# Softmax numerators kept in fp32 against an fp32 value table in a two-layer attention kernel

## The chip, the cores and the metric

The kernel runs on one core of one Trainium2 chip. The metric is the device time of one execution in microseconds (us); the engines meant below are PE (TensorE, with its weight loads shown apart as PEld), DVE (VectorE), ACT (ScalarE), POOL (GpSimd) and SP (SyncE, which here only issues transfers).

## The reference

Two batches of 1024 rows with 256 features pass through two layers. Each layer is an attention of 16 heads (16 features a head) over 77 keys, and then a feed-forward part. The part that matters here is the attention:

```python
attn = jax.nn.softmax(jnp.einsum('bqhd,bkhd->bhqk', q, k) * scale, axis=-1)   # layer 0
out = jnp.einsum('bhqk,bkhd->bqhd', attn, v).reshape(B, T_q, D_MODEL)
...
scores = scores + distance_bias[:, None, :, :]                                # layer 1
attn = jax.nn.softmax(scores, axis=-1)
out = jnp.einsum('bhqk,bkhd->bhqd', attn, v)
```

Layer 0's feed-forward part is a pair of products with ternary weights (256 to 1024 to 256, with GELU); layer 1's is one dense expert of the same sizes with ReLU, followed by a layer norm.

## The kernel before

**Units.** The 2048 rows are worked in 8 units of 256 rows (`NU = 8`, `UR = 256`). The program is written engine by engine, with semaphores between the engines; each engine runs its instructions strictly in the written order.

**Slots.** A layer's attention is a software pipeline, written out in `attn_slot(l, s)` on every engine. Slot `s` computes the score maxima of unit `s`, the scores and exponentials of unit `s-1` (three of five parts, the other two in slot `s+1`), the values product of unit `s-2`, the transposed outputs and the output projection of unit `s-3`, and the layer norm's factors and what follows for unit `s-4`. Within a slot six steps `r = 0..5` interleave these. On PE the slot ends with `values(l, s-2, 0)`, the transposes of the maxima (`shifts_transposed`), and `values(l, s-2, 1)`. Layer 0's last slots are interleaved with the ternary part, and layer 1's first three slots with the end of it; layer 1's last slots are interleaved with the expert (`expert_hidden`, `expert_out`), which then runs alone to the end.

**Heads packed by keys.** The 8 heads of a half have 8 x 77 = 616 key columns, padded to 5 tiles of `KR = 124` (`TPH = 5`). A part `r` of the scores is two such tiles by 256 rows, `psD`, 124 x 512. Both halves make 10 tiles, 5 parts a unit.

**Numerators, before.** ACT writes the exponential of a part to `p32` (a ring of four parts, L716), and copies it to fp16, `ph` (`high`, L725). POOL subtracts and rounds the rest to fp16, `pl` (`plo`, L498). `exponent` waits until POOL has read the ring's slot (`plo` of part n-4); `high` and `plo` wait until the values product of unit u-2 is done (`ppv`), since `ph` and `pl` are double buffered by unit. The profile's names for them are `p`, `pp_hi` and `pp_lo`.

**Values product.** The numerators are the stationary operand (124 x 128), and a small table of values (124 x 34 or 124 x 51: two or three heads of 16 features and a column for the sum) is the moving one. The table too is split in two fp16 parts, `vo` and `vlo`, written by DVE in `tables_v` (L938). For each of two groups of 128 rows there are 10 tiles with three products each, L1431, L1433 and L1434: 60 matmuls a unit.

**What follows.** DVE divides (`divide`, L1099 and L1100), PE transposes (L1510), ACT and DVE split the result to fp16 halves (L674, L1128), PE projects (L1448), DVE adds the residual (L1072) and takes the layer norm's statistics (L881 to L886), POOL computes the factors (`factors`, L400 to L417), ACT applies them (L689). In layer 0 DVE then works out the quantisation scales (L1045 to L1049). The scores' operand `qb` is laid out by transfers that SP issues (L293, L307), the last of them the shift rows from `mT` (L317), which come from the transposed maxima (PE L1520, ACT L707).

The fp16 halves of the numerators share their memory with the expert's hidden activations (`ehT`).

Of the kernel before, what the change touches and what calls it, by code (L numbers as in the profile page):

```python
# [23 lines left out]
ALU = mybir.AluOpType  # L24
# [45 lines left out]
def build(nc, io):  # L70
    es = ExitStack()
    with es:
# [68 lines left out]
        vo = sb("vo", [KR, B, 2, TPH, SLOTS, VW], F16)  # L141
        vlo = sb("vlo", [KR, B, 2, TPH, SLOTS, HD], F16)
# [21 lines left out]
        ehT = [t[:, 0:2 * FK * UR].rearrange("p (a c r) -> p a c r", a=2, c=FK) for t in pp]  # L164
# [74 lines left out]
        A = [Stage(f"a{l}", "pq pm pmT psc ppv poT pwo pxT qhi qlo mx mTc exp phi plo norm oTh oTl res fac app xn dq q1 xTh xTl")  # L239
# [134 lines left out]
        def _(pool):  # L374
# [115 lines left out]
            def plo(l, u, r):  # L490

                a = A[l]
                if not 0 <= u < NU:
                    return
                n = 5 * u + r
# [51 lines left out]
        def _(act):  # L547
# [162 lines left out]
            def exponent(l, u, r):  # L710

                a, n = A[l], 5 * u + r
                if 0 <= u < NU:
                    act.wait_ge(a["psc"], n + 1)
                    ge(act, a["plo"], n - 3)
                    a_(p32[:, n % 4, :, :], psD[n % 2][0:KR, :].rearrange("p (t r) -> p t r", t=2),  # L716
                       ACT.Exp, scale=1.0 / SSC).then_inc(a["exp"], 1)

            def high(l, u, r):

                a, n = A[l], 5 * u + r
                if 0 <= u < NU:
# [1032 lines left out]
```

## Time and profile before

| what | value |
|---|---|
| median of 3 runs | 428.0 us (427.83, 428.0, 437.11) |
| the profiled execution, its own time | 433.62 us |
| its span in the profile | 431.9 us |
| mean granted PE clock in it | 0.92 of full speed |
| instructions in the span | 9332 |

The busy times and the groups of instructions stand with the other rows further down. In the profile's timeline and lists a row gives the duration of an instruction as the profiler recorded it. PE's instructions are pipelined: a matmul record is some 0.18 us long even where the next one starts 0.025 us later, so the pace of a run of matmuls is read from start to start, never from the mean length.

### The profile page before, as it was taken

What the parts mean: (1) busy time and instruction counts of PE and PEld (TensorE: products, weight loads), DVE (VectorE), ACT (ScalarE), POOL (GpSimd) and SP (SyncE); (2) the same over time, 40 slices, a digit from 0 to 9 for tenths busy, and PEclk for the clock granted to TensorE, in tenths of its full rate; (3) what the DMA queues carried; (4) which work ended last, traced back from release to release, by engine and by line L of the source; (5) the groups of instructions that cost most, each with busy time, mean ns of one, the idle gap of its engine ahead of it and who ended that gap; (6) DMA issues with size and microseconds to landing.
All of it is one profiled execution on the core that took longest, in us unless ns stands there. A gap on an engine that the chain in (4) does not pass through costs nothing.

```text
span 431.9 us, 9332 instructions
## 1 busy us (share of the span) xinstructions
PE 333.7 (77%) x3346; PEld 269.8 (62%) x3346; DVE 309.8 (72%) x663; ACT 282.7 (65%) x515; POOL 233.1 (54%) x414
## 2 busy tenths in 40 slices
PE   4858657876768656757866689999868899999990
PEld 4636445765655334444654568777767789888880
DVE  6965726888887776799977553678866648777775
ACT  2147666878988668997952675877677655555520
POOL 4664554366778511457664744765587144544443
PEclk9986766899999689888989998999999999999996
DMA  8965122111110000000054222221100000000001
GB/s 237 278 93 180 27 62 77 29 30 30 39 40 22 0 2 1 2 0 2 8 153 128 48 50 49 49 49 44 44 11 2 2 2 27 26 26 25 26 26 49
DMA packets 34213, 21.48 MB, mean 50 GB/s; under 512 B 10359, under 2 KB 33528, under 8 KB 34091
## 3 DMA queue, kind: packets, MB, share of 16 engines
q1 hardware_dynamic: 32440, 20.41, 17.6%
q10 hardware_dynamic: 1728, 0.47, 0.8%
q8 instruction: 27, 0.44, 0.4%
q14 instruction: 18, 0.15, 0.1%
HBM read 10.34 MB, written 2.10 MB: 29 GB/s over the span
## 4 chain that ended last, share of the span: by engine, by line
PE 32%; DVE 26%; ACT 13%; issue 10%; POOL 7%; SPq 6%; ACTq 2%; DMA 2%; POOLq 0%; DVEq 0%
PE psA L1681 8%; PE psD L1666 4%; SPq L293 4%; PE psBE L1666 4%; DVE st L881 3%; DVE mx L1114 3%; ACT pp_hi L725 2%; DVE ham L1160 2%; POOL lns L400 2%; PE psA L1467 2%; PE psA L1448 2%; ACTq L585 2%; PE psD L1379 2%; ACT p L716 1%; DVE o L1100 1%
## 5 line engine op out<-in xcount | busy, mean ns | idle before, releaser
L498 POOL TENSOR_TENSOR pp_lo<-p,pp_hi 124x512 f16<-124x512 f32 x80 | 92.5, 1176 | 60.1 <-ACT pp_hi L725 59.9
L400 POOL TENSOR_TENSOR lns<-lns,mhalf 128x2 f32<-128x2 f32 x40 | 31.3, 782 | 114.0 <-DVE lns L886 113.7
L1114 DVE TENSOR_REDUCE mx<-psBE 128x6 f32<-128x462 f32 (+1 forms) x96 | 54.5, 579 | 31.4 <-PE psBE L1405 31.2
L716 ACT ACTIVATE p<-psD 124x512 f32<-124x512 f32 x80 | 47.7, 598 | 36.2 <-PE psD L1379 32.0
L1379 PE MATMUL psD<-qb,ktb 98*124 98x256 f16 (+1 forms) x256 | 49.4, 290 | 5.2 <-DMA qb<-mT 3.6
L725 ACT ACTIVATE pp_hi<-p 124x512 f16<-124x512 f32 x80 | 50.4, 630 | 0.0
L1379 PEld LDWEIGHTS psD<-qb,ktb 98*124 98x124 f16 (+1 forms) x256 | 34.1, 145 | 9.4 <-DMA qb<-mT 6.7
L1405 PE MATMUL psBE<-kt_hi,q_hi 128*128 128x308 f16 (+2 forms) x128 | 34.7, 313 | 4.1 <-DVE mx L1114 2.7
L1431 PE MATMUL psA<-vo,pp_hi 124*128 124x34 f16 (+1 forms) x320 | 28.0, 183 | 11.1 <-DVE xT_lo L906 4.8
L1681 PE MATMUL psA<-ew_hi,pp_lo 128*128 128x256 f16 x128 | 34.9, 273 | 0.0
L1681 PE MATMUL psA<-ew_hi,pp_hi 128*128 128x256 f16 x128 | 34.9, 273 | 0.0
L1681 PE MATMUL psA<-ew_lo,pp_hi 128*128 128x256 f16 x128 | 34.9, 273 | 0.0
L1431 PEld LDWEIGHTS psA<-vo,pp_hi 124*128 124x128 f16 x320 | 26.0, 97 | 14.2 <-issue 14.1
L1199 DVE TENSOR_TENSOR pp_lo<-space,pp_hi 128x512 f16<-128x512 f32 x32 | 23.4, 750 | 15.5 <-ACT space L827 15.4
L571 ACT ACTIVATE xT_hi<-psA 128x512 f16<-128x512 f32 x24 | 14.2, 593 | 23.2 <-PE psA L1285 23.2
L825 ACT ACTIVATE pp_hi<-psD,b1s 128x256 f16<-128x256 f32 x32 | 15.7, 491 | 19.7 <-PE psD L1666 19.7
L1434 PE MATMUL psA<-vo,pp_lo 124*128 124x34 f16 (+1 forms) x320 | 27.9, 182 | 0.0
L1433 PE MATMUL psA<-vlo,pp_hi 124*128 124x32 f16 (+1 forms) x320 | 27.8, 181 | 0.0
L881 DVE BATCH_NORM_STATS2 st<-xs 128x6 f32<-128x256 f32 x64 | 23.8, 414 | 3.0 <-DMA xs<-in_x 2.7
L1433 PEld LDWEIGHTS psA<-vlo,pp_hi 124*128 124x128 f16 x320 | 25.6, 97 | 0.3
L1376 PE MATMUL psD<-bb,selb 128*124 128x256 f16 x80 | 21.5, 279 | 5.2 <-DMA qb<-mT 5.2
L1434 PEld LDWEIGHTS psA<-vo,pp_lo 124*128 124x128 f16 x320 | 25.5, 97 | 0.0
(203 smaller groups left out, 1109.9 us busy)
## 6 DMA issues: line engine op xcount, KB each, us to landing
qb<-q_hi SPq DMA_DIRECT2D x128, 32.0 KB
xs<-in_x SPq DMA_DIRECT2D x8, 256.0 KB, 5.2
tw_raw<-in_tw SPq DMA_DIRECT2D x2, 1024.0 KB, 8.8
qb<-q_lo SPq DMA_DIRECT2D x64, 32.0 KB
space<-in_ew SPq DMA_DIRECT2D x2, 1024.0 KB, 6.5
out<-space SPq DMA_DIRECT2D x8, 256.0 KB, 2.1
qb<-bT_lo SPq DMA_DIRECT2D x8, 104.0 KB
space<-in_distN SPq DMA_DIRECT2D x1, 616.0 KB
```

Of the source, the lines that this page charges most:

```text
L400: nc.gpsimd.tensor_tensor(lns[:, n % 4, 1, :], lns[:, n % 4, 0, :], mhalf[:, :], ALU.pow).then_inc(s_rs, 1)
L498: nc.gpsimd.tensor_tensor(pl[:, u % 2, 2 * r:2 * r + 2, :], p32[:, n % 4, :, :], ph[:, u % 2, 2 * r:2 * r + 2, :], ALU.subtract).then_inc( ...
L716: a_(p32[:, n % 4, :, :], psD[n % 2][0:KR, :].rearrange("p (t r) -> p t r", t=2), ACT.Exp, scale=1.0 / SSC).then_inc(a["exp"], 1)
L725: a_(ph[:, u % 2, 2 * r:2 * r + 2, :], p32[:, n % 4, :, :], ACT.Copy).then_inc(a["phi"], 1)
L881: i = v.bn_stats(st[:, n % 4, j, :], src[:, j, :])
L1114: v.tensor_reduce(mx[:, s % 2, j * H + 6 * k:j * H + 6 * k + hn], psBE[:, n % 2, 0:hn * KEYS].rearrange("p (h k) -> p h k", h=hn), AX.X, A ...
L1379: i = mm(o, ktb[0:rows, hf * B + b, g, (t - g) * KR:(t - g + 1) * KR], qb[0:rows, u % NQ, hf, g, :], start=first, stop=(k == 1 and g == mi ...
L1405: i = mm(psBE[:, n % 2, o0 * KEYS:(o0 + c1 - c0) * KEYS], q[0][:, u % 2, hf, j * 128:(j + 1) * 128], kt[:, hf, b, c0 * KEYS:c1 * KEYS], st ...
L1431: mm(o, p_, w.rearrange("p s c -> p (s c)"), start=(hf == 0 and t == 0), stop=False, skip_group_check=True)
L1433: mm(ov[:, :, 0:HD], p_, wl, start=False, stop=False, skip_group_check=True)
L1434: i = mm(o, pl[:, u % 2, hf * TPH + t, rows_], w.rearrange("p s c -> p (s c)"), start=False, stop=(hf == 1 and t == TPH - 1), skip_group_c ...
L1681: i = mm(o, ehT[x_][:, u % 2, c, j * 128:(j + 1) * 128], ew2[w_][:, c, :], start=(j == 0 and c == 0 and x_ == 0 and w_ == 0), stop=(j == 1 ...
```

## The change

The numerators stay in fp32. ACT's exponential writes straight to a buffer of two units (`pp`, 2 x 10 tiles x 256 rows, whose rows 0 to 123 are `p32`), the fp16 copy on ACT and the subtraction on POOL are gone, and with them the semaphores `phi` and `plo`. The values table is one fp32 table, `vo`, and `vlo` is gone. The values product is one matmul of fp32 by fp32 for each tile and group of rows: 20 a unit. `exponent` now waits for `ppv` of unit u-2, and `values` for the five exponentials. The expert's `ehT` becomes a view of the same buffer.

```diff
-        vo = sb("vo", [KR, B, 2, TPH, SLOTS, VW], F16)
-        vlo = sb("vlo", [KR, B, 2, TPH, SLOTS, HD], F16)
+        vo = sb("vo", [KR, B, 2, TPH, SLOTS, VW])
...
-        p32 = sb("p32", [KR, 4, 2, UR])
-        pp = [sb(f"pp_{p}", [128, 2 * 2 * TPH * UR], F16) for p in ("hi", "lo")]
-        ph, pl = [t[0:KR, :].rearrange("p (a t r) -> p a t r", a=2, t=2 * TPH) for t in pp]
+        pp = sb("pp", [128, 2, 2 * TPH * UR])
+        p32 = pp[0:KR, :, :].rearrange("p a (t r) -> p a t r", t=2 * TPH)
...
-        ehT = [t[:, 0:2 * FK * UR].rearrange("p (a c r) -> p a c r", a=2, c=FK) for t in pp]
+        ehT = [pp[:, :, i * FK * UR // 2:(i + 1) * FK * UR // 2].bitcast(F16).rearrange("p a (c r) -> p a c r", c=FK)
+               for i in (0, 1)]
...
-            def plo(l, u, r):
-                ...
-                pool.wait_ge(a["phi"], n + 1)
-                ge(pool, a["ppv"], 2 * (u - 1))
-                nc.gpsimd.tensor_tensor(pl[:, u % 2, 2 * r:2 * r + 2, :], p32[:, n % 4, :, :],
-                                        ph[:, u % 2, 2 * r:2 * r + 2, :], ALU.subtract).then_inc(a["plo"], 1)
...
-                plo(l, s - 2, 2)
                 if 0 <= s - 4 < NU:
                     factors_act((1 + 2 * l) * NU + s - 4, (1.0, SX)[l], A[l]["fac"])
-                for u, r in ((s - 2, 3), (s - 2, 4), (s - 1, 0), (s - 1, 1)):
-                    plo(l, u, r)
...
                     act.wait_ge(a["psc"], n + 1)
-                    ge(act, a["plo"], n - 3)
-                    a_(p32[:, n % 4, :, :], psD[n % 2][0:KR, :].rearrange("p (t r) -> p t r", t=2),
+                    ge(act, a["ppv"], 2 * (u - 1))
+                    a_(p32[:, u % 2, 2 * r:2 * r + 2, :], psD[n % 2][0:KR, :].rearrange("p (t r) -> p t r", t=2),
                        ACT.Exp, scale=1.0 / SSC).then_inc(a["exp"], 1)
-
-            def high(l, u, r):
-                ...
-                    act.wait_ge(a["exp"], n + 1)
-                    ge(act, a["ppv"], 2 * (u - 1))
-                    a_(ph[:, u % 2, 2 * r:2 * r + 2, :], p32[:, n % 4, :, :], ACT.Copy).then_inc(a["phi"], 1)
...
-                for p in (0, 1):
-                    src = (psG, psX)[l][0:KR, p * 240:(p + 1) * 240].rearrange("p (t s d) -> p t s d", t=TPH, s=SLOTS)
-                    i = v.tensor_tensor((vo, vlo)[p][:, b, hf, :, :, 0:HD], src,
-                                        vm[:, :, :].unsqueeze(3).to_broadcast([KR, TPH, SLOTS, HD]), ALU.mult)
+                src = (psG, psX)[l][0:KR, 0:240].rearrange("p (t s d) -> p t s d", t=TPH, s=SLOTS)
+                v.tensor_tensor(vo[:, b, hf, :, :, 0:HD], src,
+                                vm[:, :, :].unsqueeze(3).to_broadcast([KR, TPH, SLOTS, HD]), ALU.mult).then_inc(s_vo, 1)
...
-                    pe.wait_ge(a["phi"], 5 * u + 5)
-                    pe.wait_ge(a["plo"], 5 * u + 5)
+                    pe.wait_ge(a["exp"], 5 * u + 5)
...
-                        p_ = ph[:, u % 2, hf * TPH + t, rows_]
-                        mm(o, p_, w.rearrange("p s c -> p (s c)"), start=(hf == 0 and t == 0), stop=False,
-                           skip_group_check=True)
-                        mm(ov[:, :, 0:HD], p_, wl, start=False, stop=False, skip_group_check=True)
-                        i = mm(o, pl[:, u % 2, hf * TPH + t, rows_], w.rearrange("p s c -> p (s c)"), start=False,
+                        i = mm(psV[:, j, h0 * VW:(h0 + hn) * VW], p32[:, u % 2, hf * TPH + t, rows_],
+                               vo[:, b, hf, t, 0:hn, :].rearrange("p s c -> p (s c)"), start=(hf == 0 and t == 0),
                                stop=(hf == 1 and t == TPH - 1), skip_group_check=True)
```

No instruction changes its place beside the others; what is gone leaves the rest in order. On PE, the first tiles of the first values product of layer 0 (unit 0, rows 0 to 127) stood so before, right behind the last score maxima of the slot; `psA` holds the output, `pp_hi` and `pp_lo` are the fp16 halves, and the semaphores waited for stand in brackets:

```order
130 L1405 MATMUL psBE<-kt_hi,q_hi 128x308 [waits mx_a0]
131 L1431 MATMUL psA<-vo,pp_hi 128x34 [waits plo_a0,xTl_l0,phi_a0,s_vo]
132 L1433 MATMUL psA<-vlo,pp_hi 128x2x16
133 L1434 MATMUL psA<-vo,pp_lo 128x34
134 L1431 MATMUL psA<-vo,pp_hi 128x51
135 L1433 MATMUL psA<-vlo,pp_hi 128x3x16
136 L1434 MATMUL psA<-vo,pp_lo 128x51
```

The same place with the change, where `pp` is the fp32 buffer:

```order
130 L1379 MATMUL psBE<-kt_hi,q_hi 128x308 [waits mx_a0]
131 L1400 MATMUL psA<-vo,pp 128x34 [waits xTl_l0,exp_a0,s_vo]
132 L1400 MATMUL psA<-vo,pp 128x51
133 L1400 MATMUL psA<-vo,pp 128x34
134 L1400 MATMUL psA<-vo,pp 128x51
135 L1400 MATMUL psA<-vo,pp 128x34 x2
```

Nothing moved; three matmuls of a tile became one, and the waits for `phi` and `plo` became one for the exponentials.

On ACT, a stretch of slot 5 of layer 0 before, from the copy `xT_hi` (step 1) to the first of the two normalisations (step 3):

```order
95 L743 ACTIVATE xT_hi<-psA,epsc 128x2x256 [waits pxT_a0]
96 L716 ACTIVATE p<-psD 124x512 [waits plo_a0,psc_a0]
97 L725 ACTIVATE pp_hi<-p 124x512 [waits ppv_a0,exp_a0]
98 L674 ACTIVATE oT_hi<-psA 128x512 [waits pwo_a0,poT_a0]
99 L600 ACTIVATE wo_hi<-wspace 128x512 [waits d_wo1]
100 L716 ACTIVATE p<-psD 124x512 [waits plo_a0,psc_a0]
101 L725 ACTIVATE pp_hi<-p 124x512 [waits ppv_a0,exp_a0]
102 L689 ACTIVATE xn<-xs,lns 128x256 [waits fac_a0]
```

and with the change:

```order
71 L719 ACTIVATE xT_hi<-psA,epsc 128x2x256 [waits pxT_a0]
72 L701 ACTIVATE pp<-psD 124x512 [waits ppv_a0,psc_a0]
73 L659 ACTIVATE oT_hi<-psA 128x512 [waits pwo_a0,poT_a0]
74 L585 ACTIVATE wo_hi<-wspace 128x512 [waits d_wo1]
75 L701 ACTIVATE pp<-psD 124x512 [waits ppv_a0,psc_a0]
76 L674 ACTIVATE xn<-xs,lns 128x256 [waits fac_a0]
```

The copies to `pp_hi` are gone from between the others, and the exponential has taken over their wait for `ppv`.

## Rows read from the trace of the kernel before

**Rows 1.** The page: busy time, share and instructions of each engine.
```profile
PE 333.7 (77%) x3346; PEld 269.8 (62%) x3346; DVE 309.8 (72%) x663; ACT 282.7 (65%) x515; POOL 233.1 (54%) x414
```

**Rows 2.** Stages: start:end, length, busy PE, PEld, DVE, ACT, POOL, clock, DMA share, GB/s.
```profile
58.00:71.00 13.00, 7.32 (x88) 6.40 (x89) 7.00 (x17) 8.90 (x17) 4.82 (x5) 0.67 0.14 38
...
109.00:121.00 12.00, 9.51 (x126) 7.97 (x125) 10.26 (x24) 11.03 (x22) 8.14 (x12) 1.00 0.15 36
...
285.40:297.35 11.95, 11.14 (x135) 9.07 (x134) 9.51 (x20) 8.47 (x18) 7.54 (x13) 1.00 0.18 42
```

**Rows 3.** The page's groups for what the change removes (busy, mean ns, idle before).
```profile
L498 POOL TENSOR_TENSOR pp_lo<-p,pp_hi 124x512 f16<-124x512 f32 x80 | 92.5, 1176 | 60.1 <-ACT pp_hi L725 59.9
L725 ACT ACTIVATE pp_hi<-p 124x512 f16<-124x512 f32 x80 | 50.4, 630 | 0.0
```

**Rows 4.** DVE's table writes (L938): count, shortest, median, longest ns.
```profile
L938 DVE TENSOR_TENSOR vlo<-psA,vm x8: 390/394/398, 35.2 to 217.8; 124x240 f16<-124x240 f32 x8
```

**Rows 5.** Timeline of PE, layer 0, first and last value matmul of a half.
```profile
90.30 0.18 PE L1431 MATMUL psA<-vo,pp_hi 124*128 124x34 f16 x1 [0.91 <-ACT pp_hi L725]
...
91.03 0.18 PE L1434 MATMUL psA<-vo,pp_lo 124*128 124x34 f16 x1
91.78 0.44 PE L1520 MATMUL psBE<-id,mx 128*128 128x128 f32 x2 [0.56 <-DVE mx L1114]
```

**Rows 6.** Weight loads of four kinds: count, shortest/median/longest ns, first and last start.
```profile
L1433 PEld LDWEIGHTS psA<-vlo,pp_hi x320: 95/96/151, 60.8 to 337.9; 124*128 124x128 f16 x160
...
L1510 PEld LDWEIGHTS psA<-id,o x64: 137/141/231, 70.2 to 339.6; 128*128 128x128 f32 x64
...
L1311 PEld LDWEIGHTS psA<-wspace,ctxT x16: 143/148/149, 15.2 to 135.0; 128*77 128x77 f32 x16
...
L1297 PEld LDWEIGHTS psA<-ctxT,wspace x16: 188/239/338, 5.4 to 122.3; 128*128 128x128 f32 x16
```

**Rows 7.** Timeline of PEld at full clock: start, length of the run, what, count.
```profile
120.35 0.47 PEld L1510 LDWEIGHTS psA<-id,o 128*128 128x128 f32 x4
...
121.42 1.09 PEld L1297 LDWEIGHTS psA<-ctxT,wspace 128*128 128x128 f32 x8
...
212.58 0.36 PEld L1330 LDWEIGHTS psA<-vsp_hi,selb 77*124 77x124 f16 x5 [0.88 <-issue]
212.86 0.36 PEld L1330 LDWEIGHTS psA<-vsp_lo,selb 77*124 77x124 f16 x5
```

**Rows 8.** Critical chain, layer 1: two places of a stretch that is all PE.
```profile
265.71 1.31 PE psA L1448 x12
...
269.95 0.24 PE psD L1379 x2
```

**Rows 9.** Timeline of PE, layer 1: where it waits, in brackets, before a row.
```profile
259.65 0.32 PE L1376 MATMUL psD<-bb,selb 128*124 128x256 f16 x1 [2.17 <-DMA qb<-mT]
...
286.09 0.27 PE L1467 MATMUL psA<-xT_hi,wq_hi 128*128 128x256 f16 x1 [0.59 <-DVE xT_lo L906]
...
290.17 0.18 PE L1431 MATMUL psA<-vo,pp_hi 124*128 124x34 f16 x1 [0.18 <-ACT pp_hi L725]
```

**Rows 10.** Critical chain of layer 1, one slot apart.
```profile
290.17 0.74 ACT q_hi L666 x2
...
297.35 0.72 POOL lns L400
...
302.08 0.74 ACT q_hi L666 x2
```

**Rows 11.** Quantisation scale in layer 0 (DVE L1049): shortest/median/longest ns.
```profile
L1049 DVE TENSOR_SCALAR dq<-am,ws x8: 209/998/1007, 90.3 to 173.1; 128x2 f32<-128x2 f32 x8
```

**Rows 12.** Timeline of ACT and of PE in layer 0's third slot.
```profile
55.31 0.60 ACT L716 ACTIVATE p<-psD 124x512 f32<-124x512 f32 x1 [3.43 <-POOL pp_lo L498]
...
60.84 0.19 PE L1431 MATMUL psA<-vo,pp_hi 124*128 124x34 f16 x1 [4.81 <-DVE xT_lo L906]
...
63.42 0.88 PE L1285 MATMUL psA<-id,xn 128*128 128x128 f32 x3
```

More of the change, by code:

```diff
@@ L231, in __getitem__ @@
                 return self.s[n]
-        A = [Stage(f"a{l}", "pq pm pmT psc ppv poT pwo pxT qhi qlo mx mTc exp phi plo norm oTh oTl res fac app xn dq q1 xTh xTl")
+        A = [Stage(f"a{l}", "pq pm pmT psc ppv poT pwo pxT qhi qlo mx mTc exp norm oTh oTl res fac app xn dq q1 xTh xTl")
              for l in (0, 1)]
@@ L487, in _ @@
             diag(id16, 1.0)
-            def plo(l, u, r):
[L492 to L495, printed above, removed]
-                pool.wait_ge(a["phi"], n + 1)
-                ge(pool, a["ppv"], 2 * (u - 1))
-                nc.gpsimd.tensor_tensor(pl[:, u % 2, 2 * r:2 * r + 2, :], p32[:, n % 4, :, :],
-                                        ph[:, u % 2, 2 * r:2 * r + 2, :], ALU.subtract).then_inc(a["plo"], 1)
             def attn_slot(l, s):
-                plo(l, s - 2, 2)
                 if 0 <= s - 4 < NU:
                     factors_act((1 + 2 * l) * NU + s - 4, (1.0, SX)[l], A[l]["fac"])
-                for u, r in ((s - 2, 3), (s - 2, 4), (s - 1, 0), (s - 1, 1)):
-                    plo(l, u, r)
             for s in range(NU + 4):
@@ L737, in attn_slot @@
                         exponent(l, u, k)
-                        high(l, *((u, k - 1) if k > 0 else (u - 1, 4)))
                     if r == 1 and 0 <= s - 5 < NU:
@@ L935, in tables_v @@
                 dve.wait_ge(s_vop, 4 * l + step)
-                for p in (0, 1):
-                    src = (psG, psX)[l][0:KR, p * 240:(p + 1) * 240].rearrange("p (t s d) -> p t s d", t=TPH, s=SLOTS)
-                    i = v.tensor_tensor((vo, vlo)[p][:, b, hf, :, :, 0:HD], src,
-                                        vm[:, :, :].unsqueeze(3).to_broadcast([KR, TPH, SLOTS, HD]), ALU.mult)
-                i.then_inc(s_vo, 1)
+                src = (psG, psX)[l][0:KR, 0:240].rearrange("p (t s d) -> p t s d", t=TPH, s=SLOTS)
+                v.tensor_tensor(vo[:, b, hf, :, :, 0:HD], src,
+                                vm[:, :, :].unsqueeze(3).to_broadcast([KR, TPH, SLOTS, HD]), ALU.mult).then_inc(s_vo, 1)
                 v.tensor_scalar(vo[:, b, hf, :, :, HD], vm[:, :, :], SM * SONE, None, ALU.mult).then_inc(s_vo, 1)
@@ L1329, in tables_vo @@
                         h0 = hf * HH + VH0[t]
-                        i = mm((psG, psX)[l][0:KR, p * 240 + t * 48:p * 240 + t * 48 + 48], sel[:, t * KR:(t + 1) * KR],
+                        i = mm((psG, psX)[l][0:KR, t * 48:t * 48 + 48], sel[:, t * KR:(t + 1) * KR],
                                vsp[p][:, b, h0 * HD:(h0 + SLOTS) * HD], start=(p == 0 and t == 0), stop=(p == 1 and t == TPH - 1))
@@ L1426, in values @@
                         h0, hn = hf * HH + VH0[t], VHN[t]
-                        o = psV[:, j, h0 * VW:(h0 + hn) * VW]
-                        ov = o.rearrange("p (s c) -> p s c", c=VW)
-                        w, wl = vo[:, b, hf, t, 0:hn, :], vlo[:, b, hf, t, 0:hn, :]
-                        p_ = ph[:, u % 2, hf * TPH + t, rows_]
-                        mm(o, p_, w.rearrange("p s c -> p (s c)"), start=(hf == 0 and t == 0), stop=False,
-                           skip_group_check=True)
-                        mm(ov[:, :, 0:HD], p_, wl, start=False, stop=False, skip_group_check=True)
-                        i = mm(o, pl[:, u % 2, hf * TPH + t, rows_], w.rearrange("p s c -> p (s c)"), start=False,
+                        i = mm(psV[:, j, h0 * VW:(h0 + hn) * VW], p32[:, u % 2, hf * TPH + t, rows_],
+                               vo[:, b, hf, t, 0:hn, :].rearrange("p s c -> p (s c)"), start=(hf == 0 and t == 0),
                                stop=(hf == 1 and t == TPH - 1), skip_group_check=True)
```

2 lines of the change are left out of this document (removed).

## The prediction

> **What bounds the kernel now.** I read the page's busy times first: no engine is full over the span; PE is busy 77%, DVE 72%, ACT 65%, POOL 54% [rows 1]. So the question is what sets the length of a slot, and for that I read three stretches of the table by stage [rows 2]. In a warm slot of layer 0 (109 to 121 us) ACT is busy 11.0 of 12.0 us, DVE 10.3, PE 9.5. In a slot of layer 1 (285.4 to 297.35) PE is busy 11.1 of 11.95 and nothing else is above 9.5. PE's record of a matmul is longer than its place in the pipeline, so I also count its work by pace. Twelve fp16 matmuls of 256 columns take 1.31 us, 0.109 each [rows 8]. A slot of layer 1 issues 26 such for the scores and 12 each for queries and projection (50 x 0.109 = 5.5 us), maxima of 4928 columns (2.1), ten fp32 transposes at about 0.11 (1.1; four loads take 0.47 with the last one's 0.14, [rows 6, 7]), and 60 value matmuls. Thirty of these run from 90.30 to 91.03, 0.025 us each, 1.5 for a unit [rows 5]. That is 10.2 us of 11.95. In layer 0 the same count gives 8.0, since the bias is not in its scores and maxima.
>
> The critical chain shows the loop of layer 1: from one copy of the queries at 290.17 to the next at 302.08 it is 11.9 us long, through DVE, POOL's factors (297.35) and ACT [rows 10]; PE waits in that slot for 0.59 and 0.18 us only [rows 9]. So PE is just under the bound there and a loop of small steps sits on it.
>
> **What goes.** POOL loses 80 subtractions of 1176 ns, 92.5 us, and ACT 80 copies of 630 ns, 50.4 us [rows 3], that is 5.9 and 3.15 us a unit. Little of it is on a path that lasts. Where it is: (a) in layer 0's third slot ACT stood 3.43 us for POOL's subtractions, and this reached PE's first values product, which started at 60.84 after 4.81 us of waiting [rows 12]; I take -3.3. (b) DVE's small scale product in layer 0 has a median of 998 ns and a shortest of 209 [rows 11], and its slow ones run beside POOL's subtractions, whose 1176 ns [rows 3] are near it; with those gone it may give back up to 0.8 us a unit, which goes into the layer 0 sum below. (c) DVE loses 8 table writes of 394 ns, 3.2 us [rows 4], partly under PE; with the few other small DVE steps I take -2. (d) ACT's copies before the values product: PE waits there 0.91 us in layer 0 [rows 5], 0.18 in layer 1 [rows 9].
>
> **What comes.** 20 fp32 matmuls a unit for 60 fp16 ones. No row shows an fp32 product of 128 loaded and 34 columns, so I build the price. First, how often the engine runs one. The key table's products are 8 calls in the program (4 a layer), and the profile has 16 loads of them [rows 6]: two loads and two passes a call. So a unit becomes 40 load and matmul pairs. Second, what a load costs. fp16 loads of 128 columns last 96 ns, fp32 ones of 77 columns 148, of 128 columns 188 at the least [rows 6]. The two fp32 forms differ by 40 ns for 51 columns, 0.8 ns a column; so 128 columns occupy 128 x 0.8 = about 105 ns beyond a fixed part of 85. The same fixed part leaves 11 ns for the fp16 load, which is why 0.025 apart is possible today. Third, whether loads hide. Five fp16 loads of 124 columns take 0.36 us and the next five start 0.28 behind the first [rows 7], so one comes each 0.055 us, with 48 moving columns each (one column at the pace above is 0.0004 us, so 0.02): the loads set the pace, and the moving part is hidden below them. So 40 x 0.108 = 4.3 us a unit at full clock, against 1.5: **+2.8 us a unit**, 16 units, +45 us of PE work. Lower bound: the fp32 transposes' pace of 0.11 for 128 columns with loads of 141 ns would leave 53 ns a load, 2.2 us a unit, +0.6. Upper bound: eight fp32 pairs of 154 columns start 0.129 apart [rows 7]; if load and moving part did not overlap at 34 to 51 columns, a pair would cost 0.105 + 0.035 = 0.14, 5.6 us a unit, +4.1. At half the clock a pair costs 0.21 (load of 338 ns at the longest, [rows 6]), 8.5 us a unit.
>
> The Trainium skill, page "FP8 and Floating Point Precision", section "TensorE Precision Notes", says that a true fp32 product makes four passes. If each had a load of its own, a unit would cost twice my 4.3 us and the change would be well over 40 us slower; the rows above show two loads a call. The page "TensorE: Matmul & The Clock Gate", section "Weight-path perf modes", says that the fast weight load needs 128 columns and an input that is not fp32, which speaks against this change; the gap between 96 and 188 ns agrees.
>
> **Where the +2.8 falls.** *Layer 0, unit 0:* at 60.84 to 63.42 the clock is low (0.67 over the stretch, [rows 2, 12]). The 2.6 us become up to 8.5; with the clock partly up, I take +5. *Unit 1:* +1.5. *Units 2 to 5:* the first half of the product ends before the last maximum of the slot does (PE waits 0.91 ahead of it and 0.56 behind, [rows 5]), so its +1.4 is hidden; the second half, ahead of the next slot's first maxima, adds 1.4. Against it stand (b) and the copies in ACT's full slots, about 1.4 a unit: 0 in sum. *Units 6 and 7:* +1, beside the ternary part. With (a): **layer 0 about +4**.
>
> *Layer 1, unit 0:* hidden, because PE stands 2.17 us for the shift rows' transfer [rows 9] and the chain runs through SP until then. *Unit 1:* from 259.65 to 270 the critical chain is PE alone [rows 8], +2.8. *Units 2 to 4:* PE's own count becomes 10.2 + 2.8 = 13.0 us a slot, with waits of about 0.4 say 13.4. The first of these slots begins inside the stretch without a gap, so I let it pay the whole +2.8; the others were 11.95: +1.4 each. *Unit 5:* no queries in its slot, +0.4. *Units 6 and 7:* +2.8 each on PE, less ACT's copies (3.15 a unit) ahead of the expert's first activations, together +1. From about 340 us on, PE runs the expert without a gap and nothing changes. **Layer 1 about +8.**
>
> **What costs nothing.** The exponential's new wait for `ppv` of unit u-2: PE issues the scores of unit u behind that product, so it is met whenever the scores are. If the order on PE were another, ACT would stand for up to the length of a product, 4.3 us a unit. The write of fp32 instead of fp16 by ACT has the length of L716 already. No transfer is added; SP's shift rows start when the transposed maxima are out, and what PE does meanwhile only becomes longer.
>
> **Sum.** 431.9 + 4 + 8 - 2 = 441.9 us of span, +2.3%. The profiled execution took 433.6, the median of the runs 428.0; 428.0 x 441.9 / 431.9 = **438 us**.
>
> **The rivals.** *Absorbed:* the loop without PE sets the slots, and relief on ACT, POOL and DVE (5.9 + 3.15 us a unit) pays for the PE work outside layer 1's middle slots. Then only units 1 to 4 of layer 1 cost (about +8) and the rest returns it: 428 to 434. For it: ACT's 11.0 of 12 us in layer 0. Against: PE's 13.0 us exceed 11.95. *Faster, by a cheap load:* if an fp32 load of a product costs what that of a transpose does (53 ns), PE gains 0.6 us a unit only, layer 1's slots stay at about 11.5, and (a) to (d) are left: -3 -2, some -0.5 a slot: 420. It decides at about 70 ns a pair, where PE's count meets 11.5. Against it stands the 188 ns row. *No overlap, or the clock:* at 0.14 us a pair each unit costs 1.3 us more, of which some 10 of 16 show: +13, 451. If the granted clock fell in the long runs of loads, where few columns move, one such stretch of 3.4 us in each of 12 slots would lose 1.7 us each: 458. Against: the clock is 1.00 in the slots of rows 2 with PE standing now and then.
>
> The Trainium skill, page "SBUF — State Buffer", section "Who interferes with whom", states that DVE and POOL block each other on a shared pair of ports; the 998 against 209 ns agree, and (b) would be worth all of its 0.8 us a unit by that rule, which would bring the time to about 434.
>
> **Chances.** As forecast (434 to 445) 0.45; absorbed 0.25; faster by the cheap load or by more relief than counted 0.12; no overlap or lower clock 0.18. A difference under 2% is about what a measurement of this kernel cannot tell from no change, so 419.4 to 436.6 is "same": the absorbed case, a quarter of the forecast's chance and a third of the faster case, 0.40; faster 0.08; slower 0.52. Range for 8 in 10: 424 to 454; the forecast's own is 434 to 445.
>
> **What would show it.** Right: 40 pairs a unit on PE, loads of about 190 ns, starts 0.108 apart; slots of layer 1 at 13.0 to 13.6 us with PE's waits under 0.5; DVE L1049 at 0.2; the expert's stretch as long as before. Wrong: pairs at 0.05 or 0.14 apart; PE waits as before in layer 1; a granted clock under 1.00 in layer 1's middle; slots in layer 0 shorter than 12 us, which would say that ACT's copies were the bound there.

## The result: slower by 5.9%, outside the predicted range

The changed kernel takes 456.5 us (median of four runs, 451.4 to 461.5) against 430.5 for the kernel before on the same chip: ratio 1.059, 95% interval 1.043 to 1.075. I had said 438, with 424 to 454 as the range. Executions over 1.5% above the fastest of their kernel (here 461.5) are left out of every ratio. The profiled execution took 456.45 us with a span of 454.7, 22.8 more than the span of before.

The page of the changed kernel first: busy times with instructions, the share of each engine in the chain that ended last, and the price of the new product (matmuls, then weight loads).

```profile
PE 392.7 (86%) x3026; PEld 333.6 (73%) x3026; DVE 295.0 (65%) x655; ACT 244.0 (54%) x435; POOL 140.2 (31%) x334
...
PE 64%; DVE 17%; ACT 5%; issue 4%; SPq 3%; POOL 2%; ACTq 2%; DMA 1%; DVEq 0%; POOLq 0%
...
L1400 PE MATMUL psA<-vo,pp 124*128 124x34 f32 (+1 forms) x640 | 80.8, 287 | 3.5 <-DVE xT_lo L882 3.5
...
L1400 PEld LDWEIGHTS psA<-vo,pp 124*128 124x128 f32 x640 | 80.7, 206 | 4.1 <-issue 3.8
```

Against [rows 1] POOL lost 93 us, ACT 39, DVE 15, and PE gained 59. In the chain PE had 32% before; now it has 64%. The 640 pairs are the 40 a unit that were forecast. Their loads have a median of 192 ns:

```profile
L1400 PEld LDWEIGHTS psA<-vo,pp x640: 186/192/338, 57.0 to 357.9; 124*128 124x128 f32 x160
...
L1023 DVE TENSOR_SCALAR dq<-am,ws x8: 207/208/208, 89.3 to 178.0; 128x2 f32<-128x2 f32 x8
```

The second row answers [rows 11]: DVE's small scale product is at its shortest time in all eight units.

Three slots follow, one of layer 0 and two of layer 1, in the columns of [rows 2] (start:end, length, busy PE, PEld, DVE, ACT, POOL, granted clock, DMA share, GB/s). Each runs from DVE's reciprocal of one unit's sums, about 1 us behind that unit's values product, to the next unit's. In the kernel before these slots were 12.75, 11.91 and 11.92 us long.

```profile
94.64:108.87 14.23, 14.23 (x100) 13.30 (x98) 9.50 (x23) 8.86 (x16) 2.44 (x7) 0.74 0.14 28
...
290.73:306.43 15.70, 15.70 (x116) 14.27 (x115) 9.23 (x21) 6.14 (x12) 1.90 (x7) 0.83 0.15 31
...
306.43:320.34 13.91, 13.91 (x119) 12.94 (x118) 9.13 (x20) 6.02 (x12) 1.89 (x7) 0.96 0.17 35
```

PE is busy for the whole of each. The new thing is the granted clock: 0.74, 0.83 and 0.96, where the second and third stretch of [rows 2] showed 1.00. The same table in pieces of 7 us, for PE alone (length, busy PE, clock, DMA share, GB/s), puts the fall in its place:

```profile
99.00:106.00 7.00, 7.00 (x65) 0.98 0.10 21
106.00:113.00 7.00, 7.00 (x36) 0.51 0.17 36
...
280.00:287.00 7.00, 7.00 (x65) 1.00 0.24 50
287.00:294.00 7.00, 7.00 (x33) 0.51 0.16 34
```

The clock is at 2.4 GHz in nearly all of the first piece and at 1.2 in nearly all of the second. The change falls into a values product, in layer 0 these rows of the weight loads' timeline (start, length of the run, count):

```profile
102.24 2.33 PEld L1400 LDWEIGHTS psA<-vo,pp 124*128 124x128 f32 x20
104.41 0.29 PEld L1487 LDWEIGHTS psBE<-id,mx 128*128 128x128 f32 x2
104.67 3.09 PEld L1400 LDWEIGHTS psA<-vo,pp 124*128 124x128 f32 x20
```

Ten such stretches stand in this kernel, each beginning in a values product or just behind it; six of the sixteen products have none. All in all PE is at half clock for about 103 us of the span, in the kernel before for 69 (twice the part of the mean granted clock that is missing, times the span: 0.887 of 454.7 us, 0.920 of 431.9). An estimate from these: 34 more microseconds at half speed are some 17 us of work lost, if PE is the bound in all of them. The kernel's own executions point the same way: 449.6 us of span went with a clock of 0.896, 454.7 with 0.887 and 454.8 with 0.881.

The chain of layer 1 answers [rows 10]: DVE, POOL, ACT and DMA are gone from it, and two slots read PE all through. Of that stretch:

```profile
298.50 1.31 PE psA L1415 x12
...
300.08 2.15 PE psA L1400 x20
302.24 0.25 PE psBE L1487 x2
302.49 2.58 PE psA L1400 x20
...
316.94 0.25 PE psBE L1487 x2
317.19 2.16 PE psA L1400 x20
```

Twenty pairs take 2.15 to 2.16 us, 0.108 a pair, as forecast. The 2.58 is a product in which the clock falls while it runs.

### The profile page after: what moved, and what is told of

It reads as the page before. It is cut to its first block, busy times and chain, and to the rows that moved or that the text cites. A ratio compares the mean times of both kernels' runs of the same rounds, so it can differ in the third digit from the quotient of the medians.

```text
span 454.7 us, 8391 instructions
## 1 busy us (share of the span) xinstructions
PE 392.7 (86%) x3026; PEld 333.6 (73%) x3026; DVE 295.0 (65%) x655; ACT 244.0 (54%) x435; POOL 140.2 (31%) x334
## 4 chain that ended last, share of the span: by engine, by line
PE 64%; DVE 17%; ACT 5%; issue 4%; SPq 3%; POOL 2%; ACTq 2%; DMA 1%; DVEq 0%; POOLq 0%
PE psA L1400 17%; PE psA L1648 8%; PE psD L1353 6%; PE psA L1415 5%; PE psD L1633 5%; PE psBE L1633 4%; PE psA L1434 4%; PE psBE L1379 3%; SPq L292 2%; DVE st L857 2%; PE psA L1477 2%; DVE mx L1088 2%; DVE ham L1134 2%; PE psD L1350 2%; PE psA L1259 2%
## 5 line engine op out<-in xcount | busy, mean ns | idle before, releaser
L1400 PE MATMUL psA<-vo,pp 124*128 124x34 f32 (+1 forms) x640 | 80.8, 287 | 3.5 <-DVE xT_lo L882 3.5
L1400 PEld LDWEIGHTS psA<-vo,pp 124*128 124x128 f32 x640 | 80.7, 206 | 4.1 <-issue 3.8
L701 ACT ACTIVATE pp<-psD 124x512 f32<-124x512 f32 x80 | 47.2, 595 | 66.5 <-PE psD L1353 66.1
L1648 PE MATMUL psA<-ew_hi,pp 128*128 128x256 f16 x256 | 43.1, 273 | 0.0
L1173 DVE TENSOR_TENSOR pp<-space,pp 128x512 f16<-128x512 f32 x32 | 22.0, 705 | 20.0 <-ACT space L803 20.0
L1648 PE MATMUL psA<-ew_lo,pp 128*128 128x256 f16 x128 | 34.9, 273 | 0.0
L556 ACT ACTIVATE xT_hi<-psA 128x512 f16<-128x512 f32 x24 | 14.2, 593 | 34.0 <-PE psA L1259 34.0
L801 ACT ACTIVATE pp<-psD,b1s 128x256 f16<-128x256 f32 x32 | 15.5, 484 | 22.7 <-PE psD L1633 22.7
L1648 PEld LDWEIGHTS psA<-ew_hi,pp 128*128 128x128 f16 x256 | 25.1, 98 | 2.9
L1415 PE MATMUL psA<-wo_hi,oT_hi 128*128 128x256 f16 x64 | 17.7, 277 | 3.5 <-DVE oT_lo L1102 3.4
L1134 DVE TENSOR_REDUCE ham<-space 128x1 f32<-128x1024 f32 x16 | 18.8, 1212 | 2.6 <-ACT space L757 2.6
L1601 PE MATMUL psA<-ew_hi,wspace 128*128 128x256 f16 x128 | 19.7, 321 | 0.0
```

What stands on the lines that cost most here:

```text
L701: a_(p32[:, u % 2, 2 * r:2 * r + 2, :], psD[n % 2][0:KR, :].rearrange("p (t r) -> p t r", t=2), ACT.Exp, scale=1.0 / SSC).then_inc(a["exp" ...
L1134: i = v.tensor_reduce(g[:, 0, j:j + 1], h32[:, j, :], AX.X, ALU.max, apply_absolute_value=True)
L1400: i = mm(psV[:, j, h0 * VW:(h0 + hn) * VW], p32[:, u % 2, hf * TPH + t, rows_], vo[:, b, hf, t, 0:hn, :].rearrange("p s c -> p (s c)"), st ...
L1415: i = mm(o, oT[x_][:, u % 2, c, j * 128:(j + 1) * 128], w[w_][:, c, :], start=first, stop=(j == 1 and c == DK - 1 and x_ == 1))
L1648: i = mm(o, ehT[x_][:, u % 2, c, j * 128:(j + 1) * 128], ew2[w_][:, c, :], start=(j == 0 and c == 0 and x_ == 0 and w_ == 0), stop=(j == 1 ...
```

## The experiments

All ratios are to the kernel before on the same chip, whose median was 431.9 us for e1_spread to e4_norelief, 433.4 for e5_both to e8_clock, and 432.1 for e9_poolbusy and e4_look. The theory to test was: **the clock** falls because the product is one long run of loads that move few columns, and this costs most of what I had missed. Its rival: **the work** of the 45 us on PE simply shows to a larger part than the 27 us of it that I had counted before any relief, or the relief on ACT and POOL gives less.

**The product in pieces (e1_spread).** Same work, but the 40 pairs come as four pieces of ten pairs between other matmuls.

```diff
-            def values(l, u, j):
+            def values(l, u, j, hf):
...
                         project(l, s - 3)
+                    if r >= 3 and (l, s) != (0, 2):
+                        values(l, s - 2, (r - 3) // 2, (r - 3) % 2)
...
-                values(l, s - 2, 0)
                 if s < NU:
                     shifts_transposed(l, s)
-                values(l, s - 2, 1)
+                values(l, s - 2, 1, 1)
```

> The changed kernel with the values product cut in four pieces of five tiles (10 weight loads each), issued behind steps 3, 4 and 5 of the slot and behind the transposes of the maxima, in place of two runs of 20 loads at the slot's end (layer 0's unit 0 stays at the end). The computation is the same. Theory clock: the granted clock falls because the slot's end holds a run of 4.5 us in which the array mostly loads weights; broken up, the stretches at half clock in slots 88 to 135 and 283 to 360 us (about 48 us of them) mostly go, PE gets back about half their length where it is the bound, and the time is 438 to 445 us. Theory work: the 2.8 us a unit of PE work alone sets the time, and where it stands is of no account: 453 to 459 us, whatever the clock does.

436.9 us (median of ten), 1.011 [1.007, 1.015]: 1 us under the range of the clock theory, 16 under that of the work. The two pieces of 7 us, same columns as above:

```profile
106.00:113.00 7.00, 5.56 (x53) 1.00 0.21 45
...
287.00:294.00 7.00, 7.00 (x65) 1.00 0.19 39
```

The clock stays at 2.4 GHz and 4.8 points of the 5.9 are gone. But order changed as well, so spread pairs might also hide better beneath other work; the next kernel leaves the order alone.

**More columns a load (e2_wide).** Each product moves its columns of the value table twice, the second time to accumulator columns that nobody reads. Order, waits and loads are those of the changed kernel; PE has more to do.

```diff
+                        o = bass.AP(... ap=[psV[:, j, c0:c0 + n].ap[0], [step, 2], [1, n]])
-                        i = mm(psV[:, j, h0 * VW:(h0 + hn) * VW], p32[:, u % 2, hf * TPH + t, rows_],
-                               vo[:, b, hf, t, 0:hn, :].rearrange("p s c -> p (s c)"), ...
+                        i = mm(o, p32[:, u % 2, hf * TPH + t, rows_],
+                               vo[:, b, hf, t, 0:hn, :].rearrange("p s c -> p (s c)").unsqueeze(1).to_broadcast([KR, 2, n]), ...
```

> The changed kernel with each product of numerators and table moving its 34 or 51 table columns twice, the second copy into columns of the PSUM bank that nothing reads. The output is the same; loads, their number and their place are the same, only twice the columns move below them (68 or 102 columns, 57 or 85 ns at full clock, still under the load's 105). Theory clock, by moving columns: pairs still start 0.108 apart, the clock stays at 2.4 GHz through the slot's end, 438 to 445 us. Theory work: same pace, same time, 453 to 459 us. If the clock falls all the same, it is not the number of moving columns that decides.

440.0 us, 1.020 [1.013, 1.027], in the clock's range. More work on PE takes 16 us less. Its loads, the same two pieces of 7 us, and a slot of each layer:

```profile
100.55 2.31 PEld L1404 LDWEIGHTS psA<-vo,pp 124*128 124x128 f32 x20
...
106.00:113.00 7.00, 5.96 (x53) 1.00 0.20 42
287.00:294.00 7.00, 7.00 (x63) 1.00 0.10 20
...
91.20:103.80 12.60, 11.26 (x102) 10.02 (x100) 9.31 (x24) 8.55 (x17) 2.45 (x7) 1.00 0.16 33
293.14:306.23 13.09, 13.09 (x116) 12.13 (x115) 9.02 (x20) 6.03 (x12) 1.91 (x7) 1.00 0.19 40
```

Wide moving operands hide below the load (2.31 us for 20, against 2.33 in the changed kernel), the clock is 1.00, and the slots are 12.6 and 13.1 us where the changed kernel had 14.2, and 15.7 and 13.9 in layer 1's middle. Order is the same in both, so it isn't order that saved the time: the clock did, and wider products kept it.

**Both (e5_both).** If the two remedies remove the same loss, they don't add.

```diff
+                if hf == 1:
+                    i.then_inc(a["ppv"], 1)
...
+                        i = mm(o, p32[:, u % 2, hf * TPH + t, rows_], ... .to_broadcast([KR, 2, n]), ...
```

> Both measures at once on the changed kernel: the values product in four pieces along the slot and each product moving its table columns twice. The computation is the same. After the first four runs the theory is: relief on ACT and POOL gives about 21 us, the fp32 product's 2.8 us a unit takes back some 29, and the granted clock falling at the slot's end some 17 more. Either measure alone gave 437 and 440 us. If both removed the same loss (the clock), together they give no more than 3 us more: 434 to 438. If each removed a loss of its own, 418 to 424.

439.3 us, 1.014 [1.006, 1.021]: 1 us over the range for a shared loss, far from the 418 to 424 for two losses, and between the two single measures, whose intervals it overlaps. What the three kernels still lose to the one before, 1.1 to 2.0%, I put down to the work less the relief.

**The relief alone (e3_relief).** The kernel before, with the exponential written straight to fp16: no copy on ACT, no subtraction on POOL, and still 60 fp16 products (the third repeats the high half, so the low half of the numerators is left out).

```diff
-                plo(l, s - 2, 2)
...
-                for u, r in ((s - 2, 3), (s - 2, 4), (s - 1, 0), (s - 1, 1)):
-                    plo(l, u, r)
...
-                    ge(act, a["plo"], n - 3)
-                    a_(p32[:, n % 4, :, :], psD[n % 2][0:KR, :].rearrange("p (t r) -> p t r", t=2),
+                    ge(act, a["ppv"], 2 * (u - 1))
+                    a_(ph[:, u % 2, 2 * r:2 * r + 2, :], psD[n % 2][0:KR, :].rearrange("p (t r) -> p t r", t=2),
...
-                        high(l, *((u, k - 1) if k > 0 else (u - 1, 4)))
...
-                        i = mm(o, pl[:, u % 2, hf * TPH + t, rows_], w.rearrange("p s c -> p (s c)"), start=False,
+                        i = mm(o, p_, w.rearrange("p s c -> p (s c)"), start=False,
```

> The kernel before with the relief alone: the exponential writes fp16 numerators directly, no copy on ACT, no subtraction on POOL; PE keeps its 60 fp16 matmuls a unit, the third of each tile taking the high half in place of the low one (so the low halves of the numerators are left out of the computation, and the third product repeats the first). Prediction's own theory: the relief is worth about the items (a) to (d), 5 to 9 us off, 420 to 425 us. Rival: PE and the small-step loop leave it nothing, 427 to 431. Other rival: ACT and POOL were the real bound of layer 0, 405 to 415 us, and then the fp32 product's price was far over what the sum says.

411.0 us, 0.951 [0.946, 0.956]: the relief is worth 21 us, against the 5 to 9 I expected here. A slot of each layer:

```profile
82.92:93.92 11.00, 8.57 (x122) 7.40 (x120) 9.30 (x23) 8.42 (x17) 2.45 (x7) 1.00 0.16 38
...
275.55:286.49 10.94, 10.49 (x136) 9.29 (x135) 8.93 (x21) 6.02 (x12) 1.91 (x7) 1.00 0.21 48
```

The seven slots of layer 0 fell from 12.7 to 11.0 us on average and those of layer 1's middle from 11.9 to 10.9. That the latter fell at all contradicts a step of mine: I had called the copies worth 0.18 us there, by PE's wait. In the chain of the kernel before, the copy stands once in each slot of layer 1, just ahead of the queries' copies on the same engine, and [rows 10] had left it out:

```profile
301.46 0.62 ACT pp_hi L725
302.08 0.74 ACT q_hi L666 x2
```

With it gone, something else sets the 10.9 us. The chain of e3_relief names SP's queue all through this slot, and SP's timeline shows why:

```profile
275.08 5.17 SPq L293 DMA_DIRECT2D qb<-q_hi  x8
280.29 0.88 SPq L307 DMA_DIRECT2D qb<-bT_lo  x1
281.21 3.39 SPq L293 DMA_DIRECT2D qb<-q_lo  x4
284.65 1.44 SPq L317 DMA_DIRECT2D qb<-mT  x2
286.19 1.34 SPq L293 DMA_DIRECT2D qb<-q_hi  x2
```

SP hands out one DMA after the other, back to back from one slot into the next: 15 of them make a slot. Fourteen last 0.6 to 0.9 us each, and one of the four `q_lo` lasts 1.5, for a reason that the trace does not give.

**The product alone (e4_norelief, e4_look).** The changed kernel, with copy and subtraction kept on scratch tiles of four pieces and waited for where the kernel before waited; what they write is not used.

```diff
+        dh = sb("dh", [KR, 4, 2, UR], F16)
+        dl = sb("dl", [KR, 4, 2, UR], F16)
...
+                nc.gpsimd.tensor_tensor(dl[:, n % 4, :, :], p32[:, u % 2, 2 * r:2 * r + 2, :],
+                                        dh[:, n % 4, :, :], ALU.subtract).then_inc(a["plo"], 1)
...
+                    a_(dh[:, n % 4, :, :], p32[:, u % 2, 2 * r:2 * r + 2, :], ACT.Copy).then_inc(a["phi"], 1)
...
-                    pe.wait_ge(a["exp"], 5 * u + 5)
+                    pe.wait_ge(a["phi"], 5 * u + 5)
+                    pe.wait_ge(a["plo"], 5 * u + 5)
```

> The changed kernel with ACT's 80 fp16 copies and POOL's 80 subtractions put back on scratch tiles that no result depends on, with their waits; PE still runs the fp32 product and waits for them as before. Price of PE's part alone. If the relief was worth 5 to 9 us in the changed kernel: 461 to 466 us. If it was worth next to nothing since PE is the bound: 456 to 459. If it hid most of the price: over 470.

479.8 us, 1.110 [1.104, 1.116]: over 470, which was to mean a relief that hides most of the price. The execution traced here took 637.7 us at a mean clock of 0.54 and says nothing of the others, so the kernel's trace is that of a further execution:

> The kernel with the fp32 product and ACT's and POOL's parts kept, once more for its trace: 478 to 482 us. With a product of 4.6 us on PE at the slot's end and the subtractions ahead of it, PE should wait for POOL or ACT before the product in every slot, and the granted clock should be at half in more of the span than in the changed kernel (104 of 454 us there).

That single run took 469.4 us, below the interval that I had given for it, on another chip. Its span of 467.2 us has 104 at half clock, about as many as the changed kernel and not more, as I had expected; so the sum of the clock's loss comes with the product and not with the relief. PE's waits for POOL or ACT before each product, which I had expected too, are not among its longest. The low stretches lie elsewhere, though: through layer 1's middle, with the same run of 40 pairs in slots of 13.4 us, the clock is kept (PE alone, columns as above):

```profile
240.00:339.00 99.00, 90.03 (x750) 1.00 0.26 63
```

POOL again stands for the copies (column: releaser, then total us, times, longest):

```profile
POOL dl L498 <- ACT dh L725: 97.7, 29, 13.4
```

The product without relief, its clock included, is thus 37 to 48 us, and the relief in the presence of the fp32 product 13 to 23 us, a third to a half of it and not most; by the other way round (changed kernel against e3_relief) the product is 45 to 46. The parts add up within these bounds.

**Which part of the relief (e6_nopool).** The kernel before without POOL's subtractions only; ACT's copies stay, and the ring of exponentials waits for them.

```diff
-                plo(l, s - 2, 2)
...
-                    ge(act, a["plo"], n - 3)
+                    ge(act, a["phi"], n - 3)
...
-                    pe.wait_ge(a["plo"], 5 * u + 5)
```

> The kernel before with POOL's subtractions alone left out (the low halves of the numerators are left out of the computation; the third product of a tile repeats the high half, so PE has its 60 matmuls). ACT still copies to fp16. Splits the relief of 21 us. If it was POOL (its queue ahead of the layer norm's factors, and DVE's small steps beside it): 411 to 417 us. If it was ACT's copies: 425 to 431. By the busy times gone (92.5 us on POOL, 50.4 on ACT) it would be about 418.

418.6 us, 0.966 [0.959, 0.973]: 15 of the 21 us are POOL's, and what is left, 6, falls to the copies. Is it that someone waits for POOL, or that POOL is busy?

**POOL busy, nobody waits (e9_poolbusy).** e6_nopool with 80 subtractions of the same size put back, reading a constant tile. Neither the exponentials nor the values product of PE waits for them, and nobody uses what they write. The diff is against the kernel before.

```diff
-                nc.gpsimd.tensor_tensor(pl[:, u % 2, 2 * r:2 * r + 2, :], p32[:, n % 4, :, :],
-                                        ph[:, u % 2, 2 * r:2 * r + 2, :], ALU.subtract).then_inc(a["plo"], 1)
+                nc.gpsimd.tensor_tensor(pl[:, u % 2, 2 * r:2 * r + 2, :].rearrange("p t (a b) -> p (t a) b", b=128),
+                                        ones32[0:KR, :].unsqueeze(1).to_broadcast([KR, 4, 128]), ...
+                    ge(act, a["plo"], 5 * (u - 1))
```

> The kernel without POOL's part (418.6 us, against 433 for the kernel before) with 80 subtractions of the same size put back on POOL in the old places, from a constant tile and the high half into the unused low half, so that neither the exponential's ring nor PE's product waits for them. (The low halves of the numerators are left out of the computation; the third product of a tile repeats the high half.) Splits POOL's 15 us. If what cost was the waits for POOL's result (the ring, the product): 417 to 420 us. If it was POOL being busy (its queue ahead of the layer norm's factors, and DVE's small steps held up beside it, 5.7 us in sum by the traces): 426 to 433.

429.2 us (ten runs), 0.996 [0.992, 1.001]. Of the 15 us, 11 (by medians) to 13 (by ratios) come back. Three small DVE operations, first in e6_nopool, then in e9_poolbusy with the subtraction (busy us, mean ns, idle before), and the spread of the first (shortest/median/longest ns):

```profile
L1046 DVE TENSOR_SCALAR dq<-am,ws 128x2 f32<-128x2 f32 x8 | 1.7, 207 | 0.0
L1043 DVE TENSOR_SCALAR am<-am 128x2 f32<-128x2 f32 x8 | 1.4, 170 | 0.3
L1045 DVE RECIPROCAL am<-am 128x2 f32<-128x2 f32 x8 | 1.3, 166 | 0.3
```

```profile
L1055 DVE TENSOR_SCALAR dq<-am,ws 128x2 f32<-128x2 f32 x8 | 4.8, 602 | 0.0
L1052 DVE TENSOR_SCALAR am<-am 128x2 f32<-128x2 f32 x8 | 4.1, 510 | 0.3
L1054 DVE RECIPROCAL am<-am 128x2 f32<-128x2 f32 x8 | 1.3, 166 | 0.3
L498 POOL TENSOR_TENSOR pp_lo<-ones,pp_hi 124x512 f16<-124x512 f32 x80 | 92.6, 1178 | 57.7 <-ACT pp_hi L730 57.6
...
L1055 DVE TENSOR_SCALAR dq<-am,ws x8: 207/600/1003, 87.8 to 171.9; 128x2 f32<-128x2 f32 x8
```

So a busy POOL holds DVE up with nobody waiting on a semaphore, and not in every operation: the reciprocal between the two keeps its 166 ns. The two stretched rows explain 5.8 us over layer 0's eight units, if all of it lies on the path that lasts; the rest of the 11 to 13 lies in other small steps (the norm's scale, L886 before, had a mean of 224 ns and 179 in e6_nopool) and in steps of POOL itself, which stand behind the subtractions in its queue. I did not separate these. Nor did I separate the clock: e9_poolbusy is at half clock for 81 us of its span and e6_nopool for 66 (mean clock 0.906 and 0.921), so a part may have come through PE. A few waits that keep the buffers safe between units remain in e9_poolbusy, so its 11 to 13 us are rather an upper bound for being busy alone.

**Fewer products (e7_relief40).** e3_relief with two fp16 products a tile instead of three (the numerators are fp16 only).

```diff
-                        mm(ov[:, :, 0:HD], p_, wl, start=False, stop=False, skip_group_check=True)
-                        i = mm(o, p_, w.rearrange("p s c -> p (s c)"), start=False,
-                               stop=(hf == 1 and t == TPH - 1), skip_group_check=True)
+                        i = mm(ov[:, :, 0:HD], p_, wl, start=False, stop=(hf == 1 and t == TPH - 1), skip_group_check=True)
```

> The relief-only kernel with two fp16 products a tile in place of three (high half of the numerators against the table's high and low part, the low halves of the numerators are left out of the computation): 40 fast loads a unit, 0.5 us of PE work less a unit. If PE's work counts at about two thirds of its length, as the fp32 product showed (29 of 45 us), 16 x 0.5 x 0.65 = 5 us off 411: 404 to 408. If the loop without PE sets the slots now, 409 to 412.

409.7 us, 0.938 [0.930, 0.946], faster than both kernels. The four times are 405.1, 406.5, 412.9 and 413.8, and the ratio goes by the first two. By it the 20 products less a unit give 1.3 points over e3_relief, 5 to 6 us, which is the range for PE's work counting at two thirds. The traced execution is the one of 413.8, and its middle slots are as long as those of e3_relief (11.0 and 11.35 us in layer 0, 10.96 and 11.25 in layer 1), which fits a slot that SP's queue sets. These runs do not decide between the two. This version keeps both fp16 halves of the value table, but only the high half of the numerators.

**The clock by itself (e8_clock).** Only PE runs: 192 load and matmul pairs of fp32 with 128 loaded columns, behind 44 fp16 matmuls of 512 columns each time; the moving columns are 34, 51, 68, 102 and 128, and two runs are fp16. Nothing of the kernel is computed.

```diff
+            def f32(cols, n):
+                for k in range(n):
+                    i = mm(ps[:, 1, 0:cols], xs[:, k % 8, 0:128], xs[:, 8, 0:cols], start=True, stop=True)
...
+            fill()
+            f32(34, 96)
+            fill()
+            f32(51, 96)
+            fill()
+            f32(68, 96)
```

> Computes nothing of the reference (the output is a copy of x): PE alone, runs of about 21 us of one kind of matmul, each behind 44 fp16 matmuls of 512 columns: fp32 with 34, 51, 68 and 102 moving columns, then fp16 with fast loads and 34 and 128 columns, then fp32 with 128. If the clock follows how much of the time columns move, it falls in the fp32 runs of 34 and 51 columns and stays in those of 102 and 128, and the fp16 run of 34 columns at 0.025 us a matmul keeps it. If any run of fp32 products lets it fall, all five do. Starts are 0.108 us apart up to 102 columns in either case at full clock, and 0.21 at half.

Rows of PE alone (length, busy, granted clock, DMA share, GB/s): fp32 with 34 columns (the first two), 51 (two), 68, 102, fp16 with 34, fp32 with 128. It is one execution, with the runs in this order.

```profile
20.80:27.00 6.20, 6.20 (x56) 0.99 0.01 3
27.00:56.20 29.20, 29.20 (x138) 0.50 0.00 1
68.00:85.00 17.00, 17.00 (x153) 1.00 0.01 1
85.00:93.60 8.60, 8.60 (x42) 0.50 0.01 2
105.50:126.90 21.40, 21.40 (x193) 1.00 0.00 1
136.40:157.80 21.40, 21.40 (x193) 1.00 0.00 1
167.30:182.70 15.40, 15.28 (x602) 1.00 0.02 4
...
218.30:239.90 21.60, 21.60 (x194) 1.00 0.01 2
```

With 34 and 51 moving columns, the kernel's two sizes, PE falls from 2.4 to 1.2 GHz within the run, 6 us after its start with 34 columns and 17 with 51, and stays there to its end, though it is busy without a gap; with 68 and 102 (those of e2_wide) it does not. In the kernel the clock falls within a product of some 5 us or just behind it, among other work on PE; that the product brings it there rests on e1_spread and e2_wide, not on this run. At full clock a pair takes 0.112 us with 68 columns as with 102. fp16 loads with 34 moving columns, 0.0255 us a pair, kept the clock too; the products of the kernel before are of that kind.

## Why the prediction failed

**The parts.** Changes against the kernel before, in us, from the profiled executions: layer 0 up to DVE's reciprocal behind its last values product (155.3 before), from there to the one behind layer 1's last (338.2), the rest, and the span (431.9).

| kernel | layer 0 | layer 1 | rest | span |
|---|---|---|---|---|
| relief alone, e3_relief | -17.3 | -4.7 | 0 | -22.0 |
| and the fp32 product at a kept clock, e2_wide | -3.2 | +7.6 | 0 | +4.4 |
| the changed kernel | +4.6 | +15.5 | +2.7 | +22.8 |

From line to line: relief -22, product +26, clock +18.5. e2_wide kept the clock better than the kernel before did (39 us at half clock against 69), but e1_spread and e5_both, with 64 and 65, end at +3.4 and +4.4 us of span too, so the 4 us do not hang on that.

**The clock** is the step that failed: the sum had no term for a lower clock outside layer 0's first unit, and it cost 18.5 us. The prediction had it as a rival, priced at 458 us (456.5 measured) for the right reason, and gave it and "no overlap" 0.18 together. That the number came so near is partly luck: it stood for twelve stretches of 3.4 us, and there are ten, most of them 6.8 us long. It was argued down with "the clock is 1.00 in the slots of rows 2 with PE standing now and then". That row shows the clock under fp16 loads of 0.025 us a pair, not under a run of 0.108 us each; it could say nothing about a load that takes four times as long for the same columns. No row of before shows such a run. The low clock of the third slot [rows 2] was in view and was read as given for the first unit alone. The remedy kernels put its price at 17 (e2_wide) to 21 us (e1_spread), by the ratios.

**The price of the product** was right. 40 pairs a unit, loads at 192 ns, 0.108 us apart: all three as worked out from [rows 6, 7], though the slope of 0.8 ns a column was a line through two kinds of load only, which might have missed. How much of it shows in the time was right too: the terms come to 13 us in layer 0 and 14 in layer 1 before any relief is taken off, 27 in all, against 14 and 12, 26 in all, measured. (The layer 1 terms as written add to 9.8 net, and the text rounded them to 8; this hid 2 us.) The slots of layer 1 were to be 13.4 us, and at a kept clock they are 13.1. The Trainium skill, page "TensorE: Matmul & The Clock Gate", section "Weight-path perf modes", which takes the fast load away from fp32, stood the test: 192 against 96 ns.

**The relief** was counted too small: some -15 us in all (3.3, then 1.4 in each of four units, 4.6 for the copies at layer 1's end, 2 on DVE) against -22. In layer 0 e3_relief gained 5.1 us up to the first unit's reciprocal, where (a) had 3.3, and then 1.7 a slot in all seven, where I took ACT's copies and DVE's small step as 1.4 in four. (b), though, was the right mechanism, at 207 ns in all eight units, and a second step, L1046, was held as well (403 ns on average before, 170 without the subtractions). In layer 1's middle I took nothing, because I priced the copy by PE's wait of 0.18 us for it [rows 9]; it stood on the loop's chain with 0.62, and the three slots there gained 2.7 together. At layer 1's end I took too much, 4.6 against 2.0. Alone all this would have made the forecast some 6 us too high.

**"What costs nothing"** held at a kept clock: in e2_wide the time behind layer 1's last reciprocal is the same as before within 0.1 us. In the changed kernel the expert's stretch, which I had said would be as long as before, is 88.7 us instead of 85.8, since the low clock behind the last product reaches into it (columns of [rows 2]):

```profile
358.30:447.00 88.70, 84.95 (x748) 74.65 (x746) 60.83 (x116) 45.92 (x120) 39.32 (x73) 0.96 0.06 19
```

**The rivals.** "Absorbed" and "faster" fell with the measured 13.1 us slots, "no overlap" with pairs 0.108 us apart. Yet absorption was nearly true without the clock: relief and work differ by 4 us.

**What stays open.** Whether POOL's own queue, DVE's held steps or PE's clock carry the larger part of the 11 to 13 us; what PE's work is worth once ACT and POOL are relieved (e7_relief40); and why six of the sixteen products, and those of layer 1's middle in e4_look, kept the clock. That e4_look was 10 us shorter than e4_norelief goes with the clock: 0.889 against 0.86 to 0.87 is 104 us at half clock against 124 to 134. None of this touches the verdict on the clock.

## What to carry to other kernels

Before trading many cheap matmuls for fewer dear ones, look at how many columns follow each weight load: a row at full clock vouches only for its own mix of loads and moving columns, and the clock can cost nearly as much as the work (here 18.5 us against 26). Where loads set the pace and the columns are few, break the run up between other matmuls, or widen the moving operand, which hides below the load. Price the relief of a side engine by the chain and by what it blocks, not by the wait of the busiest engine, and look at which queue is next in line before spending more on PE.

## What the runs showed of the chip

- PE, busy without a gap, fell from 2.4 to 1.2 GHz in the runs of fp32 products with 34 and 51 moving columns (0.99 then 0.50, 1.00 then 0.50) and stayed at 1.00 in those with 68, 102 and 128. "Busy 100%" on the page doesn't mean that the clock is kept.
- The moving part of an fp32 pair is hidden up to 128 columns: 21.55 us for 192 pairs with 68 columns, 21.58 with 102 and 21.60 with 128.
- POOL's subtractions (1.18 us each) stretch a DVE operation of 128x2 from 207 to as much as 1003 ns, while a reciprocal of the same size keeps its 166, and cost the kernel 11 to 13 of 432 us with nearly nobody waiting for their result. The Trainium skill, page "SBUF — State Buffer", section "Who interferes with whom", has DVE and POOL block each other on a shared pair of ports; the 1003 ns agree.
- SP's queue of DMA issues, 15 in a slot and most of them 0.6 to 0.9 us long, is the chain of a slot of layer 1 (10.9 us) once ACT and POOL are relieved. In the kernel before they took some 10 of the 11.9 us and were not in such a slot's chain. No run took transfers away to test it.
